# Moving a table lookup, a wait on the load queue, two bias additions, five filler products and one score stage in a block of attention between two routed networks

## The reference, cut to what matters

```
x = x + 0.5 * ffn(layernorm(x))     # ffn(n=0)
x = x + attention(layernorm(x))     # 16 heads of 16, 64 landmarks
x = x + 0.5 * ffn(layernorm(x))     # ffn(n=1), same weights

def ffn(x):
    shared = (silu(x @ sg.T) * (x @ su.T)) @ sd.T
    logits = x @ gate.T                       # 8 experts
    top, score = argmax(logits), sigmoid(max(logits))
    routed = for each token: expert[top] on x * score
    return shared + routed

def attention(x):
    q, k, v = ...; q_l, k_l = means of q and k over groups of 8
    s1 = softmax(q @ k_l.T); s2 = softmax(q_l @ k_l.T); s3 = softmax(q_l @ k.T)
    z = iterative pseudo-inverse of s2, 6 steps
    return (s1 @ (z @ (s3 @ v))) @ Wo + bo
```

## Time and profile before

| | us |
|---|---|
| median of three runs | 1120.60 |
| lowest, highest | 1117.92, 1121.84 |
| the profiled execution, its own time | 1117.92 |
| its span in the profile | 1116.1 |
| TensorE busy | 1070.7 (96%) |
| VectorE, ScalarE, GpSimd busy | 732.9, 552.7, 532.2 |
| stages, from the span's start: n = 0 shared part, n = 0 tiles | 0 to about 171, to about 376 |
| attention: opening, loop | 376 to 418, to about 740 |
| n = 1 shared part, n = 1 tiles | to about 907, to 1116 |

### The profile page before, as it was taken

The page is one execution under the profiler, slowest core; times in us unless marked ns, Lnnn a source line. Parts: engine busy times, 40 slices in busy tenths (PEclk is TensorE's granted clock), DMA queues, the critical chain, the costliest instruction groups (busy, mean ns, idle before and its releaser), DMA issues.

```text
span 1116.1 us, 29694 instructions
## 1 busy us (share of the span) xinstructions
PE 1070.7 (96%) x11336; PEld 853.0 (76%) x11337; DVE 732.9 (66%) x1379; ACT 552.7 (50%) x919; POOL 532.2 (48%) x746
## 2 busy tenths in 40 slices
PE   7999999999999899999999999999999999999996
PEld 5788887888876677777767777768888887788864
DVE  5736746767664387878878868756347566766752
ACT  4344335666654355456455555343443256666641
POOL 5720544666665462452553541326201726666662
PEclk9999999999999999999999999999999999999998
DMA  7273035232224220000000000105241142322232
GB/s 265 76 263 153 19 127 177 69 123 70 74 72 147 88 77 3 3 4 3 3 3 3 3 2 4 41 2 208 95 170 38 68 164 75 127 73 69 67 109 79
DMA packets 41204, 89.77 MB, mean 80 GB/s; under 512 B 5876, under 2 KB 30583, under 8 KB 40064
## 3 DMA queue, kind: packets, MB, share of 16 engines
q1 hardware_dynamic: 30160, 62.41, 15.7%
q0 software_dynamic: 10368, 25.19, 7.2%
q10 hardware_dynamic: 560, 0.52, 0.1%
HBM read 65.03 MB, written 26.21 MB: 82 GB/s over the span
## 4 chain that ended last, share of the span: by engine, by line
PE 76%; DVE 11%; ACT 4%; issue 4%; DMA 2%; POOL 1%; ACTq 0%; DVEq 0%; POOLq 0%; SPq 0%
PE PS L1960 15%; PE PS L1874 11%; PE PS L1974 10%; PE PS L1890 7%; PE PS L2099 3%; PE PS L1967 3%; PE PS L1805 2%; PE PS L1986 2%; PE PS L2219 2%; PE PS L2232 2%; PE PS L1908 2%; ACT XNT L1380 2%; DVE A_NM L887 1%; PE PS L2253 1%; PE PS L1901 1%
## 5 line engine op out<-in xcount | busy, mean ns | idle before, releaser
L1960 PE MATMUL PS<-WHL,XGH 128*128 128x512 f32 x528 | 182.9, 427 | 0.7 <-DVE WHL L748 0.7
L1707 POOL TENSOR_TENSOR A_W<-A_XC,CB 128x256 f32<-128x256 f32 x86 | 61.8, 737 | 150.8 <-DVE A_XC L992 150.8
L1974 PE MATMUL PS<-WD,XNT 128*128 x528 | 126.7, 383 | 1.7 <-issue 1.0
L1276 ACT ACTIVATE XNT<-PS,SCORES 128x512 f32<-128x512 f32 x72 | 49.6, 688 | 142.3 <-PE PS L1960 120.4
L1614 POOL DMA_INDIRECT X<-xs_dram,WHO x72 | 91.5, 1270 | 55.2 <-issue 26.6
L1608 POOL TENSOR_SCALAR XNT<-WD 128x128 f32<-128x128 f32 x64 | 52.0, 832 | 129.5 <-DVE WD L639 129.5
L1960 PEld LDWEIGHTS PS<-WHL,XGH 128*128 128x128 f32 x528 | 94.1, 189 | 17.5 <-issue 1.5
L1974 PEld LDWEIGHTS PS<-WD,XNT 128*128 128x128 f32 x528 | 95.2, 190 | 15.1 <-issue 3.7
L1890 PE MATMUL PS<-SDH,HHL 128*128 128x256 f32 x512 | 103.4, 286 | 2.4 <-DVE X L680 2.2
L1960 PE MATMUL PS<-WHL,XGL 128*128 128x512 f32 x264 | 104.3, 395 | 0.0
L697 DVE TENSOR_TENSOR HHL<-HSB,HHL 128x512 fp32r<-128x512 f32 x64 | 46.2, 722 | 80.3 <-ACT HHL L1237 80.3
(11 more groups left out here) (300 smaller groups left out, 2618.5 us busy)
## 6 DMA issues: line engine op xcount, KB each, us to landing
xs_dram<-WG SPq DMA_DIRECT2D x16, 512.0 KB, 3.0
WU<-in_r_up SPq DMA_DIRECT2D x2, 4096.0 KB
shared_dram<-X SPq DMA_DIRECT2D x16, 512.0 KB, 3.1
WG<-in_r_gate SPq DMA_DIRECT2D x2, 4096.0 KB
WD<-in_r_down SPq DMA_DIRECT2D x4, 2048.0 KB
X<-in_x SPq DMA_DIRECT2D x7, 512.0 KB, 9.4
X<-mid_dram SPq DMA_DIRECT2D x7, 512.0 KB, 3.9
X<-in_r_gate SPq DMA_DIRECT2D x6, 512.0 KB
```

Of the source, the lines that this page charges most:

```text
L1276: act.activation(B["RS"][:, u * F:(u + 1) * F], banks[1 + u % 2][:], ACT.Silu, scale=B["SCORES"][:, bass.ds(t if tile is None else tile, 1 ...
L1707: pool.tensor_tensor(B["W"][:].rearrange("p (a m) -> p a m", m=M)[:, part, :], B["XC"][b % 2][:].rearrange("p (a w) -> p a w", w=XW)[:, pa ...
L1960: ins = pe.matmul(banks[bank][:], tok, w[:, k * F:(k + 1) * F], start=(k == 0 and i == 0), stop=(k == KD - 1 and i == 2))
L1974: ins = pe.matmul(banks[7][:, 0:D], B["HT"][:, u * F + f * P:u * F + (f + 1) * P], B["WD"][:, bass.ds(ex * (KF * D) + f * D, D)], start=(f ...
```

## The change

It does six things. (1) `find_experts` moves from slot 26 to slot 27, directly ahead of `read_table`. (2) The load queue no longer waits for nine tiles before it loads the first second expert. (3) On GpSimd both `add_bias(0)` and `add_bias(1)` come ahead of `s2_normalise(0)`. (4) `add_bias(1)` leaves the loop's first turn. (5) `fill(1, 8)` becomes `fill(1, 3)`. (6) `first_s1_max(1)` with its wait comes after `s3_turned(0, 0)` on TensorE, not ahead of it. VectorE's and ScalarE's order in attention stays as it was.

```diff
-                        tile_hot=22, owners=23, scores=24, find_experts=26, read_table=27)
+                        tile_hot=22, owners=23, scores=24, read_table=27)
...
             need(sp, "x_out_last", 16 * (NG - PARTS_G))
-            need(sp, "ry_ready", UNR * UNR)
             for i in range(UNR):
...
-                    elif slot == ROUTING_SLOT["find_experts"]:
+                    elif slot == ROUTING_SLOT["read_table"]:
                         find_experts()
-                    elif slot == ROUTING_SLOT["read_table"]:
                         read_table()
...
             batch_normalise(1)
+            add_bias(0)
+            add_bias(1)
             s2_normalise(0)
-            add_bias(0)
             batch_root(2)
...
-                if b == 0:
-                    add_bias(1)
                 if exists(far):
                     add_bias(far)
...
-            fill(1, 8)
+            fill(1, 3)
             pe.wait_ge(att["s3m"], count("s3m", 0, 4))
             turn_nm3(0)
...
             project_qk(1, 0)
-            pe.wait_ge(att["s1m"], count("s1m", 0, 1))
-            first_s1_max(1)
             pe.wait_ge(s_picks, 5)
             pe.wait_ge(att["s2s"], count("s2s", 0, 1))
             s3_turned(0, 0)
+            pe.wait_ge(att["s1m"], count("s1m", 0, 1))
+            first_s1_max(1)
             project_qk(1, 1)
```

## The result

The changed kernel took 1126.3 us (median of 6 executions, 1123.3 to 1128.8), the kernel before beside it 1118.8 us (1117.9 to 1121.8). The ratio is 1.006, 95% interval 1.0038 to 1.0083: **slower, by about 7 us**. The forecast was 1121.3 us. The profiled execution took 1124.7 us with a span of 1122.9 us, 6.8 us more than before's span.

The account below looks back on a forecast made before the run. The prediction took TensorE, with 76% of the chain, to bound the kernel. Its terms, 0.4 - 1.3 + 1.1 + 0.0 + 0.5 = +0.7 us, on the median 1120.6 us gave 1121.3 us, range 1117.5 to 1125.0.

Parts of the forecast that it names:

- The lookup: Slots 27 and 28, both feed-forward layers: VectorE's product and ScalarE's L1237 start later, +0.4 us, between 0 and 0.7.
- The burst's old place: Tiles around 230 and 970 us: the second expert's three loads no longer delay a gather there, 1.3 us given back.
- The burst in n = 1: First tiles of n = 1: the moved loads delay the first gather_residual, +1.1 us, bounds nothing and 3.2 us.
- The burst in n = 0: First tiles of n = 0: 1.9 us of room hides the delayed gather, nothing; 1.3 us if three gathers are hit.
- Fewer fillers: Opening of attention: TensorE gains about 0.2 us at turn_nm3, VectorE between nothing and 0.35 us; taken as nothing.
- The bias additions: GpSimd's idle time ahead of s2_normalise(0): no gain, but VectorE's L872 beside them takes 0.78 us and ends 0.35 us later.
- The score stage: Opening of attention: L901 starts 0.5 us late and delays turn_rows; +0.5 us with fills and additions, between -0.35 and +0.9.
- the burst costs more in n = 1, and n = 0 as well: Slower rival, first tiles: residual, residual and scatter all late in n = 1, n = 0 too; 1125.4 us, chance 0.05.
- the fall of the clock in the opening: Slower rival, attention's opening: fewer fills leave TensorE idle and its clock drops to 1.2 GHz; 1126.7 us, chance 0.05.
- three signs named against the prediction: Opening clock below 1.00 behind the fills; TensorE standing over 3 us for gathers in the first tiles; turn_rows sooner.

Follow-up runs that it names:

- e4: The kernel before with only find_experts moved from slot 26 to slot 27; ratio 1.0006 to the kernel before.
- e6: The kernel before with only fill(1, 8) changed to fill(1, 3); ratio 1.0030 to the kernel before.
- e10: The kernel before with fill(1, 3) for fill(1, 8) and five products put ahead of the opening's first wait for rows; ratio 0.9998.
- e7: The kernel before with the bias additions and the score stage moved, eight filler products kept; ratio 1.0012.
- e15: The changed kernel with the load queue's wait for nine tiles put back and fill(1, 8) again; ratio 1.0013 to the kernel before.
- e3: The kernel before with only the attention opening's edits: bias additions moved, fill(1, 3) for fill(1, 8), score stage moved; ratio 1.0025.
- e14: The changed kernel with fill(1, 8) again, the load queue's wait still gone; ratio 1.0042 to the kernel before.
- e18: The kernel before without the load queue's wait, with 24 products of 16 columns added on TensorE in attention's opening; ratio 1.0050.

## Why the prediction was wrong, step by step

- **The lookup, +0.4 us: the right place, a smaller size.** ScalarE's cast now waits for VectorE's product, as forecast, but TensorE's wait behind it grew from 0.39 us to 0.45 only. n = 1's shared part grew by 0.1 us. e4's 1.0006 can't be told from nothing. L670 (L669 after) follows the low part of slot 27, as said.
- **The burst's old place, 1.3 us given back: right** (0.5 and 0.8 us, in the rows around 230 and 970).
- **The burst in n = 1, +1.1 us: right for the gather, too small for the stage.** The gather took 3.85 us where 3.9 was said. The tiles of n = 1 took 204.1 us on average in the seven profiles without the wait, 202.7 in the ten with the wait of nine: 1.4 us more with the 0.8 given back already in it, so 2.2 us for the burst at its new place, or 1.6 where the clock did not fall. That the wait for the gather can pull the clock down was left out here too.
- **The burst in n = 0, "nothing" with a bound of 1.3 us: this step failed.** It took the delay of a gather, 1.06 us, from a place where the burst had been issued 3.4 us before it, and set it against 1.9 us of room. In n = 0 burst and gather are issued in the same moment, since the queue and GpSimd wait for the same stores, and the gather took 4.3 us more (188.30 - 181.07 against 184.33 - 181.37, its issue before). The prediction had named about 4 us as the price if a gather had to wait for the whole burst, and read the 1.06 us as a sign against it. At this distance the gather pays that price: in all eight traces without the wait VectorE's addition begins within 1.8 us of the burst's last packet. No run tells whether the engines took turns there. The room was overrun. The step also looked at one path only, TensorE's down product. The scatter and the token gather stand behind the same addition on GpSimd, and they made the second wait. And it gave the wait no price in clock, 2.1 us. Together 5.0 us.
- **Fewer fillers, "I take nothing": this step failed too.** I had asked what they hide in their own place, and there TensorE gained 0.6 us at turn_nm3 where 0.2 was said, and nothing of it was lost. I had not asked what instructions that are taken away do to all that come after them. e6 and e10 show it: 1.0030 against 0.9998, 3 us for the numbers of the instructions, in stops for late blocks of the program.
- **The bias additions:** the 0.78 us for L872 did not come, since GpSimd reached the additions too late to meet it; and they had no price that can be told (e7, e15).
- **The score stage, +0.5 us: wrong in sign, small in size.** L899 was expected 0.5 us late and was 0.15 us early. The 0.6 us that the fillers gave back at turn_nm3 had been taken as 0.2, since L872 was to be slow; they outweigh the delay.

Two slower rivals had the number, by luck (1126.3 us measured): "the burst costs more in n = 1, and n = 0 as well" (1125.4 us) and the fall of the clock in the opening (1126.7 us). The first left out both the clock and the numbers of the instructions. As to the second, the clock did fall more, but in the tiles; behind the fills it stayed at 1.00. Two of the three signs named against the prediction came true: TensorE stood for gathers in the first tiles by more than 3 us (2.5 and 1.4 us in n = 0), and turn_rows came sooner than before (0.25 us).

What stays open: why some blocks of the program are fetched late, when the clock falls behind a wait and when it does not, and how 24 products in one tile raise its mean. No version was faster than the kernel before.

## What to carry to other kernels

A wait on a load queue that seems to wait for nothing may hold a transfer off the moment in which all engines depend on one small gather; price its removal by issuing it at the same instant as that gather, follow every engine that queues behind the gather, and add the clock if TensorE will stand. When a profile can't settle a difference, compare the mean granted clock of all timed executions. When instructions are removed from a long unrolled stream, compare the places of unexplained stops before judging the edit, and repeat it with as many instructions put back elsewhere: 0.3% came from their number alone.

## What the runs showed of the hardware

- TensorE stopped in the middle of runs of one line, waiting for no engine, for 0.7 to 1.7 us, on a grid of 256 of its recorded instructions. For each step of the grid an instruction queue moves one packet of 16 KB, which makes 64 bytes for an instruction (an estimate from the two). TensorE goes on 2.15 us after the packet's start at the soonest. In e3 from 700 to 716, for three steps of the grid:
```profile
q8 instruction: 3, 0.05, 1.3%
```
- Whether the clock falls behind such waits differs between executions: behind two waits of 1.3 and 2.0 us it stayed at 1.00 in e14, behind 1.3 and 2.0 us it fell to 0.50 in e18. It cost these tiles 2.1 us.
- A gather of 128 rows beside a burst of 1.5 MB, from its issue to VectorE's addition behind it: 5.9 to 7.2 us when both were issued in the same moment (n = 0, eight traces), 3.8 to 4.1 us when it was issued 2.9 us behind the burst (n = 1, seven traces), 2.8 to 3.5 us with no burst beside it.
